# A one-core Macaron block: four early iterations with slots of their own, constants in two groups, and moved slots in the loop

## The reference

```python
x = x + 0.5 * ffn(layernorm(x))       # FFN 0
x = x + mamba(layernorm(x))           # with its own residual and layernorm inside
x = x + 0.5 * ffn(layernorm(x))       # FFN 1, same weights

def ffn(x):    # 8 experts of width 176, top 2 by router, softmax of the two logits
    top_logits, idx = top_k(x @ Wg, 2);  w = scatter(softmax(top_logits))
    y = sum_e w[:, e] * ((silu(x @ W1[e]) * (x @ W2[e])) @ W3[e])
    return y + (silu(x @ Ws1) * (x @ Ws2)) @ Ws3        # shared part, width 352

def mamba(x):  # inner width 256, 16 states, convolution over 4 taps
    x_in, z = split(x @ W_in + b_in)
    xc = silu(conv(x_in) + conv_b);  B, C = split(xc @ W_xp + b_xp)
    delta = softplus(xc @ W_dt + b_dt)
    h_t = exp(delta_t * A) * h_(t-1) + delta_t * xc_t * B_t    # per state, along the sequence
    y = sum_s h_t * C_t + D_skip * xc
    return ln(x + (y * silu(z)) @ W_out + b_out) * alpha + beta
```

## Time and profile before

| | us |
|---|---|
| median of 3 runs (lowest, highest) | 1952.55 (1949.0, 1955.74) |
| the profiled execution | 1954.8 |
| its span | 1953.0 |
| PE busy | 1685.0 (86%) |
| DVE busy | 1528.1 (78%) |
| POOL busy | 1435.9 (74%) |
| ACT busy | 1216.9 (62%) |

### The profile page before, as it was taken

How to read it: one execution, slowest core, us unless ns; L and a number is a source line. 1 busy time by engine, 2 the same in 40 slices (tenths; PEclk the granted TensorE clock), 3 DMA queues, 4 the chain that set the end, 5 groups by cost and what they waited for, 6 DMA issues and landing times.

```text
span 1953.0 us, 27826 instructions
## 1 busy us (share of the span) xinstructions
PE 1685.0 (86%) x7378; PEld 1006.3 (52%) x7378; DVE 1528.1 (78%) x2337; ACT 1216.9 (62%) x1828; POOL 1435.9 (74%) x1350
## 2 busy tenths in 40 slices
PE   2896868999989899899989899898989999967488
PEld 1553535555545555555545555555555555544255
DVE  2237988988878888788878898888889898888732
ACT  1265657676856767586766767676676767665322
POOL 2336767788878778688877878788877878887853
PEclk9897969999989999999999999999999999988698
DMA  4124756776766857577665767667585867767742
GB/s 133 38 82 117 186 119 175 166 184 164 177 159 152 192 146 190 142 169 183 166 167 145 186 166 174 170 158 189 147 197 138 204 165 173 180 149 176 160 102 65
DMA packets 121342, 305.10 MB, mean 156 GB/s; under 512 B 19299, under 2 KB 40518, under 8 KB 106822
## 3 DMA queue, kind: packets, MB, share of 16 engines
q0 software_dynamic: 18432, 125.84, 31.9%
q1 hardware_dynamic: 94976, 173.07, 30.7%
q10 hardware_dynamic: 7750, 4.10, 0.8%
HBM read 167.67 MB, written 5.24 MB: 89 GB/s over the span
## 4 chain that ended last, share of the span: by engine, by line
PE 37%; issue 18%; POOL 14%; DVE 13%; DMA 11%; ACT 5%; ACTq 1%; DVEq 1%; POOLq 0%; SPq 0%
PE ps_y L1062 9%; DVE hist L903 6%; POOL prod L579 5%; POOL gated L517 5%; DMA yacc<-prod 5%; PE ps_h1b L1048 5%; PE ps_h2b L1070 5%; PE ps_h1a L1048 4%; PE ps_h2a L1070 4%; PE ps_m L1019 3%; DMA wrow<-w_rows 3%; PE ps_m L1113 3%; DMA out<-xres 2%; PE ps_m L1009 2%; DVE gated L883 1%
## 5 line engine op out<-in xcount | busy, mean ns | idle before, releaser
L579 POOL TENSOR_TENSOR prod<-hist,crow 128x1024 f32<-128x1024 f32 x224 | 566.6, 2530 | 239.6 <-DVE hist L903 237.7
L1062 PEld LDWEIGHTS ps_y<-down_w,gated 128*128 128x128 f32 (+1 forms) x3584 | 474.3, 196 | 267.4 <-issue 165.0
L903 DVE TENSOR_TENSOR_SCAN hist<-decay,ps_db 128x1024 f32<-128x1024 f32 x256 | 583.6, 2280 | 2.9
L517 POOL TENSOR_TENSOR gated<-gated,silu 128x512 f32<-128x512 f32 x352 | 484.6, 1440 | 93.9 <-DVE gated L883 81.2
L1062 PE MATMUL ps_y<-down_w,gated 128*128 128x128 f32 (+1 forms) x3584 | 489.5, 281 | 40.8 <-DVE xres L890 22.7
L855 DVE TENSOR_TENSOR ps_db<-du,ps_db 128x1024 f32<-128x1024 f32 x256 | 313.1, 1223 | 185.4 <-PE ps_db L1030 183.0
L667 ACT ACTIVATE decay<-delta,a_neg 128x510 f32<-128x510 f32 x512 | 327.0, 709 | 3.6 <-DVE hist L903 2.2
L687 ACT ACTIVATE silu<-ps_h1a 128x512 f32<-128x512 f32 (+1 forms) x224 | 133.0, 594 | 223.5 <-PE ps_h1a L1048 223.3
L1070 PE MATMUL ps_h2a<-xnT,up_w 128*128 128x512 f32 (+1 forms) x448 | 236.2, 609 | 22.9 <-DVE gated L883 22.7
L1048 PE MATMUL ps_h1b<-xnT,up_w 128*128 128x512 f32 x448 | 240.7, 619 | 3.5 <-ACT silu L687 3.5
L1070 PE MATMUL ps_h2b<-xnT,up_w 128*128 128x512 f32 x448 | 231.5, 599 | 8.5 <-DVE gated L883 8.5
(11 more groups left out here) (139 smaller groups left out, 1915.3 us busy)
## 6 DMA issues: line engine op xcount, KB each, us to landing
yacc<-prod POOLq DMA_DIRECT2D x112, 1024.0 KB, 9.4
crow<-c_rows SPq DMA_DIRECT2D x128, 512.0 KB, 4.6
wrow<-w_rows SPq DMA_DIRECT2D x320, 128.0 KB, 5.0
wrow<-w_rows SPq DMA_DIRECT2D x64, 224.0 KB, 7.2
wrow<-w_rows SPq DMA_DIRECT2D x64, 192.0 KB, 6.2
wrow<-w_rows SPq DMA_DIRECT2D x64, 160.0 KB, 2.9
yacc<-yacc POOLq DMA_DIRECT2D x16, 512.0 KB, 7.7
wrow<-w_rows SPq DMA_DIRECT2D x64, 96.0 KB, 3.5
```

The lines of the kernel that those rows point to most:

```text
L517: nc.gpsimd.tensor_tensor(gated[:, pos % NGATE, :], gated[:, pos % NGATE, :], silu[:, (pos + NCHUNK * f_parity(of, f)) % NSILU, :], ALU.mu ...
L579: nc.gpsimd.tensor_tensor(prod[:, (pair - 1 + odd) % 2, s % 2, :, :], hist[:, s % 2, :, :], c_all, ALU.mult).then_inc(prod_done, 1)
L903: nc.vector.tensor_tensor_scan(hist[:, s % 2, :, :].rearrange("p h t -> p (h t)"), decay[:, s % NA, :, :, :].rearrange("p h b t -> p (h b ...
L1062: ins = nc.tensor.matmul(ps_y[:, t * C:(t + 1) * C], gated[0:rd, posd % NGATE, t * P:(t + 1) * P], down_w[0:rd, jd, :], start=(posd == 0 a ...
```

## The change

1. The four written-out iterations -2 to 1 take `START_PLAN`, `START_UNIT` and `START_SP` in place of the three tables. Their 14 chunks of FFN 0 stand in slots 6 to 31, not 18 to 31, and the routing steps in slots 6 to 11.
2. The 23 loads are two groups: 8 for the experts on ACT's queue (`experts_loaded`) and 15 constants on SP's queue behind the load of the first group of x. TensorE starts when the 8 and 7 of GpSimd's tiles are there. GpSimd makes its other 11 tiles in slot 16 of iteration -2, DVE prepares the taps and bias parts in slot 24, and ACT and TensorE make `a_exp` and `edge_w` in slot 28.
3. In the loop `addy0` moves from slot 4 to 3, `stats1` and `scale1` one slot up, `route1` from 26 to 25, `delta` from 24 to 26, `tilt1` and `weights1` one slot up, the last chunk of FFN 1 from 16 to 17; `route0` moves from 10 to 11 and `tilt0` from 13 to 12; `w0:3` moves from 18 to 19.
4. `drop` is computed on DVE within `route`, not on GpSimd. `bparts` has no copies any more: DVE adds the bias twice, once into bf16.

```diff
     PLAN = {
-        0: ["stats0"], 1: ["scale0"], 2: ["norm0"], 3: ["fold"], 4: ["addy0", "xT0"], 5: ["stats2", "scale2", "logits0"],
+        0: ["stats0"], 1: ["scale0"], 2: ["norm0"], 3: ["addy0", "fold"], 4: ["xT0"], 5: ["stats2", "scale2", "logits0"],
...
+    START_PLAN = {s: [n for n in names if n not in ("route0", "tilt0", "weights0", "wT0")] for s, names in PLAN.items()}
+    for s, n in ((6, "route0"), (8, "tilt0"), (9, "weights0"), (11, "wT0")):
+        START_PLAN[s] = START_PLAN[s] + [n]
+    START_UNIT = {s: (0, pos) for pos, s in enumerate((6, 8, 10, 15, 16, 18, 20, 22, 24, 26, 28, 29, 30, 31))}
...
+    SETUP_MADE, SETUP_TAPS, SETUP_EDGE = 16, 24, 28
...
+            load(0, 0, 0)
+            sp.wait_ge(x_loaded, 16)
+                const(conv_w_c[:], conv_w.rearrange("(h p) o t -> p h (o t)", p=P))
+                const(taps_b, conv_w.rearrange("c o t -> (c o t)").partition_broadcast(P))
+                const(w_in[:], W_in[:, :])
...
+            for g in range(1, XS):
...
+                    if slot == SETUP_MADE and first(k):
+                        make_the_rest()
...
-                            pool.wait_ge(top_ready, route_no(k, step) + 1)
-                            nc.gpsimd.tensor_tensor(drop[:], top[:, :, 0], top[:, :, 1], ALU.subtract
-                                                    ).then_inc(drop_ready, 1)
...
+                    if slot == SETUP_EDGE and first(k):
+                        act.wait_ge(consts_loaded, 16 * N_CONSTS)
+                        nc.scalar.activation(a_exp[:], a_log[:], ACT.Exp).then_inc(a_exped, 1)
+                        act.wait_ge(edge_full, 1)
+                        nc.scalar.activation(edge_w[:], ps_m[0:PAD, 0:DI], ACT.Copy).then_inc(edge_made, 1)
...
                             dve.wait_ge(top_ready, route_no(k, step) + 1)
-                            nc.vector.memset(carrier[:], 0.0)
+                            nc.vector.tensor_tensor(drop[:], top[:, :, 0], top[:, :, 1], ALU.subtract
+                                                    ).then_inc(drop_ready, 1)
...
-                            split(chain, bc[:, :, 0:NS], brem[:], brem2[:], bparts, NS).then_inc(bparts_ready, 1)
+                            nc.vector.tensor_tensor(bc[:], rows_in, bias, ALU.add)
+                            chain.link(nc.vector.tensor_tensor(hi, rows_in[:, :, 0:NS], bias[:, :, 0:NS], ALU.add))
+                            nc.vector.tensor_tensor(brem[:], bc[:, :, 0:NS], hi, ALU.subtract).then_inc(misc_taken, 1)
+                            chain.link(nc.vector.tensor_tensor(md, bc[:, :, 0:NS], hi, ALU.subtract))
+                            chain.link(nc.vector.tensor_tensor(lo, brem[:], md, ALU.subtract))
+                            nc.vector.memset(carrier[:], 0.0).then_inc(bparts_ready, 1)
...
+                    if slot == SETUP_TAPS and first(k):
+                        prepare()
...
-            pe.wait_ge(consts_loaded, 16 * N_CONSTS)
-            pe.wait_ge(consts_made, N_MADE)
-            pe.wait_ge(taps_made, 6)
-            pe.wait_ge(b_out_made, 8)
+            pe.wait_ge(consts_made, MADE_FIRST)
+            pe.wait_ge(experts_loaded, 16 * N_EXPERTS)
```

More of the change, by code:

```diff
@@ L404, in body @@
                 for slot in range(SLOTS):
-                    for step in SP_PLAN.get(slot, []):
+                    for step in sp_plan(k).get(slot, []):
                         if step[0] == "c" and scans(k):
@@ L465, in _ @@
[L465 to L473 removed]
+            assert made == MADE_FIRST, made
@@ L884, in body @@
                                                 ).then_inc(h2_taken, 1)
-                    for step in PLAN.get(slot, []):
+                    for step in plan(k).get(slot, []):
                         if step == "addy0" and lead(k) or step == "addy1" and last(k):
@@ L980, in body @@
                             statistics(rtok, 3, mvr, stats_no(k, 3))
+                    if slot == SETUP_TAPS and first(k):
+                        prepare()
+                    if slot == SETUP_EDGE and first(k):
+                        dve.wait_ge(a_exped, 1)
+                        nc.vector.tensor_scalar(a_neg[:], a_exp[:], -1.0, None, ALU.mult).then_inc(a_ready, 1)
                     if slot == SLOTS - 1:
@@ L1138, in body @@
                             ins.then_inc(misc_full, 1)
+                    if slot == SETUP_EDGE and first(k):
+                        make_edge()
                     if slot == SLOTS - 1 and lead(k):
```

222 lines of the change are left out of this document (112 added, 110 removed), and 15 rows, old and new, of tables (PLAN, SP_PLAN, START_SP).

## The result

The changed kernel took 1895.46 us (median of 4 runs, 1892.28 to 1900.55) against 1954.14 us for the kernel before beside it: ratio 0.9704, 95% interval 0.967 to 0.9738. The forecast was 1888 us.

What follows compares the result with a forecast made beforehand. TensorE, busy for 92% of the loop, was taken to bound it. Terms of -7, -8, -6, -8, -35 and -2 made -66 against the profiled 1954.8: 1888.8, taken as 1888 us because that execution ran above the median; range 1872 to 1907.

Steps and rivals of the forecast that it cites:

- The start: Up to the first `addy0`: TensorE waits for expert loads alone, so `addy0` comes at 70.7 against 78.0 us, -7 us.
- Rival (c): The loads end no sooner and the start keeps its first 78 us: 1902 us, chance 0.04.
- Iteration -1: Before the loop: chunks between the chain's small steps fill TensorE's gaps, with its clock taken as full: -8 us.
- Iterations 0 and 1: Before the loop: with the chunks spread, DVE becomes the bound; half of the most possible gain, -6 and -8 us.
- `addy0` in slot 3: In the loop: TensorE's 1.7 us wait for `xres` before FFN 1 goes, -1.5 us in each of 12 iterations.
- The routing one slot up: In the loop: TensorE's 2.4 us wait for `wtok` goes and POOL's gates are next, -1.8 us an iteration.
- `bparts` and `drop`: DVE operations in the loop: -0.4 us from `bparts` against +0.3 from `drop` and routing waits, taken as 0 an iteration.
- The tables as a whole: Loop's moved steps: -3.3 us an iteration, less 0.4 that other waits take back, by 12 iterations: -35 us.
- `stats1`: Loop slot 19: GpSimd's last step ends earlier, so the statistics fall mostly into DVE's idle time: 0 us.
- Rival (d): Slower: in the loop the routing in slot 25, with `drop` and `hot` standing, holds up DVE; about 1966 us, chance 0.06.

## Why the prediction was right, and where it was so by luck

The measured 1895.46 us lies within the forecast's range of 1872 to 1907. (The forecast's own sum, with the 2.2 us taken off whole, is 1886.6, not 1888.)

The loop with both kinds of edit apart, in us from group 2 to 14 (in each the new start):

| | both old | `drop` on VectorE only | `bparts` new only | both new |
|---|---|---|---|---|
| old tables | 1345.6 | 1367.7 | not run | 1366.5 |
| new tables | 1334.7 | not run | 1311.2 | 1306.0 |
| old tables, ratio of the timed runs | 0.9904 | 1.007 | not run | 0.9993 |
| new tables, ratio of the timed runs | 0.9832 | not run | 0.9738 | 0.9704, 0.9694 |

The new tables are worth 11 us of the loop with both operations old (14 by the ratios), and 60 with both new (57 by the ratios). The new `bparts` is worth 15 to 18 us in the timed runs on either tables. `drop` on VectorE costs 22 us of the loop with the old tables (30 by the medians) and wins 5 to 9 with the new: it is what makes the tables' worth so different.

Where it lies within an iteration shows in the mean distance between the starts of scan j and scan j + 1 (12 iterations, worked out from the timeline; a scan is two slots). The scans whose distance differs by 0.7 us or more:

| scan | 2 | 5 | 7 | 8 | 11 | 12 | 13 | 14 | 15 |
|---|---|---|---|---|---|---|---|---|---|
| before | 8.1 | 7.2 | 6.0 | 5.6 | 8.3 | 6.5 | 7.1 | 5.6 | 10.0 |
| new tables alone | 6.7 | 6.0 | 9.6 | 5.0 | 9.0 | 6.9 | 5.8 | 7.3 | 7.3 |
| with new `bparts` | 6.6 | 6.0 | 9.4 | 5.0 | 8.0 | 6.5 | 5.8 | 7.3 | 7.2 |
| both (changed kernel) | 6.5 | 6.8 | 5.5 | 5.8 | 8.0 | 7.8 | 5.7 | 7.7 | 7.4 |

- **The start.** The order of events was right: the first chunk at 21.95 (forecast 20 to 21), the first gate at 37.4 (34.5), `addy0` at 68.2 (70.7). TensorE had waited for the last expert load until 18.45, not 16 to 17. The step from the first chunk to the gate took 15.4 us, not 14. The two table changes that the forecast put there did not come (`tilt` at 27.95 follows a Silu with no table load between), and the gate still waited 5.51 us for its rows. From the gate to `addy0` it took 30.8 us, not 36.2, and here a part is luck. With the preparation out of the way the stretch is 26.0 us, not the 29.7 carried over from before, and the work put inside costs 4.9, not the 6.5 of taps, edge weights and `sel_b` (GpSimd's first product began at 39.17, 1.1 us behind the gate's end, when `sel_b` was done). Both terms were too large, and that made up for the late gate. The gains of edits 1 and 2 overlap: by group 2, 25 of the 27 us are there with the tables of the start and all preparation in front again, and 13 with edit 2 and the old slots for the chunks. Rival (c), loads that end no sooner, is out: the wait for experts ended at 18.45, that for all 23 in before at 21.71.
- **Iteration -1.** Forecast -8, measured -6.2. The clock came as read from the earlier trace rows: 3.0 us in the first convolution.
- **Iterations 0 and 1.** Forecast -6 and -8, measured -3.2 and -7.7. The bound by VectorE's work held: it is busy for 75 of 87 and 88 of 98 us. In the first the granted clock fell (0.84 for 0.89); whether that is the missing 3 us is not shown.
- **`addy0` in slot 3.** Forecast -1.5 in an iteration, measured 19.4 by 12, or -1.6. Scan 2's distance shows it.
- **The routing one slot up.** Forecast -1.8 in an iteration, 21.6 us. This is a step that failed, in whole or in half: with it undone the profiled loop was the same, and the median 10.7 us longer. The wait for `wtok` went as foreseen and came back as a wait for GpSimd's gates, of which the prediction said that POOL "is next", without a price. The clock did not come along with it either: half clock is 30.7 us of the loop with the step and 17.1 without.
- **`bparts` and `drop`.** The mis-sized term: forecast 0, measured -28.7 under the new tables (26 by the ratios). The reading of the earlier trace rows was right, down to the subtraction that would stand in the cast's place (2.16 us); the shorter tail saves 0.27 us (forecast 0.3 to 0.5). Not seen was the last copy, 0.5 us away from GpSimd's gate, which stands for 1.77 us in every second iteration of the three kernels that have the new start and the copies. Of the 23.4 us of `bparts`, VectorE's own operations account for about 14 (4.0 us for the five old ones, 2.8 for the four new ones, by 12); another part is clock, with 64.8 us at half clock without it and 23.9 with it. That the change in the clock comes from `bparts` itself, and not from any shift of phase, is not shown, but kernels with the changed loop and another start had 23.9 and 34.1 us, so 64.8 lies outside that spread.
- **The tables as a whole.** Forecast -35 for edit 3, measured -0.5 against before or -10.9 against the start alone. Their gains are there (scans 2, 5, 13 and 15: 6.6 us an iteration), and so are four losses of the same sum: 3.6 at scan 7 from `tilt0` in slot 12 with `drop` still on GpSimd, 1.7 at scan 14 from `du`, the rest at scans 9 and 11. `drop` on VectorE removes the first, and costs 3.3 of its 3.9 us elsewhere (scans 5, 8, 12 and 14). The sum of the loop came within 6 us of the forecast because a term too large and a term too small cancelled.
- **`stats1`.** Forecast 0, and it is 0, but not for the reason given: VectorE waits 2.3 us for GpSimd, and would wait for `ps_db` otherwise.
- **Rival (d)**, the standing operations that make it slower, is true of the old tables: there `drop` on VectorE cost 22 us of the profiled loop and 30 by the medians. Its price (up to 2.3 us a time) was right, and its place depends on what GpSimd does in that slot.
